# Attention weights of a decoder layer: keys on partitions by a second score product, instead of transposed weights

## What is computed

```python
q = (x @ Wq).reshape(B, T, H, Dh)        # B = 4, T = 512, H = 16, Dh = 32
k = (x @ Wk).reshape(B, T, H, Dh)
v = (x @ Wv).reshape(B, T, H, Dh)
scores = jnp.einsum('bthd,bshd->bhts', q, k)
mask = jnp.tril(jnp.ones((T, T), dtype=scores.dtype))
scores = scores * mask
attn = jax.nn.softmax(scores / T ** 0.5, axis=-1)
out = jnp.einsum('bhts,bshd->bthd', attn, v).reshape(B, T, H * Dh)
return out @ Wo
```

## Time and profile before

| | us |
|---|---|
| median of 3 runs | 1165.44 |
| lowest, highest | 1163.69, 1166.59 |
| profiled execution | 1165.46 |
| its span | 1163.7 |
| TensorE busy | 1053.7 |
| VectorE busy | 777.4 |
| ScalarE busy | 486.3 |
| attention stage, until about | 482 |

### The profile page before, as it was taken

How to read it: one execution, slowest core, us unless ns; L and a number is a source line. 1 busy time by engine, 2 the same in 40 slices (tenths; PEclk the granted TensorE clock), 3 DMA queues, 4 the chain that set the end, 5 groups by cost and what they waited for, 6 DMA issues and landing times.

```text
span 1163.7 us, 18414 instructions
## 1 busy us (share of the span) xinstructions
PE 1053.7 (91%) x6022; PEld 844.8 (73%) x6023; DVE 777.4 (67%) x1920; ACT 486.3 (42%) x934; POOL 251.3 (22%) x431
## 2 busy tenths in 40 slices
PE   2888989898899877499999999999999999999994
PEld 1566767676677665388788888888888888888873
DVE  4678778978987998455664746655465546655666
ACT  4378638854983788122332412221132212221113
POOL 1025324523552353222221001500000000000222
PEclk9989999999999998799999999999999999999997
DMA  5797625752673482222454100510011100100001
GB/s 184 191 303 194 189 90 137 191 145 95 179 192 94 115 234 75 72 64 74 154 171 172 37 1 19 55 37 1 1 37 36 36 0 19 53 1 1 37 37 73
DMA packets 56227, 110.41 MB, mean 95 GB/s; under 512 B 6032, under 2 KB 6032, under 8 KB 56144
## 3 DMA queue, kind: packets, MB, share of 16 engines
q1 hardware_dynamic: 51504, 95.97, 29.4%
q0 software_dynamic: 4640, 13.39, 3.1%
HBM read 72.11 MB, written 35.14 MB: 92 GB/s over the span
## 4 chain that ended last, share of the span: by engine, by line
PE 55%; DVE 2%; issue 0%; ACT 0%; POOLq 0%; POOL 0%; ACTq 0%; DVEq 0%
PE f_bank L42 53%; PE f_bank L1322 1%; PE f_bank L1314 1%; PE f_bank L1364 1%; DVE rows_kept L1661 0%; DVE ln_stats L754 0%; DVE big_hi L1042 0%; DVE hs_lo L1649 0%; DVE ln_mv L756 0%; ACT L767 0%; POOLq L1108 0%; DVE h L1639 0%; ACT hs_hi L1491 0%; POOL out L1276 0%; DVE ln_shift L774 0%
## 5 line engine op out<-in xcount | busy, mean ns | idle before, releaser
L1600 DVE TENSOR_TENSOR h<-f_bank,fsg 128x512 f32<-128x512 f32 x64 | 44.3, 692 | 180.8 <-PE f_bank L42 180.7
L1468 ACT ACTIVATE fsg<-f_bank 128x512 f32<-128x512 f32 x64 | 38.3, 599 | 298.6 <-PE f_bank L42 298.5
L372 PE MATMUL bank<-ident,probs 128*128 128x128 f32 x640 | 124.0, 293 | 42.2 <-ACT probs L489 18.8
L600 DVE CUSTOM_DVE_ANT_0 bank<-bank,mask 128x384 f32<-128x384 f32 (+3 forms) x256 | 126.5, 495 | 32.7 <-PE bank L362 31.0
L489 ACT ACTIVATE probs<-bank,nmax 128x384 f32<-128x384 f32 (+3 forms) x256 | 135.4, 529 | 24.2 <-DVE nmax L610 16.0
L498 ACT ACTIVATE pt_hi<-bank 128x384 f16<-128x384 f32 (+3 forms) x256 | 112.7, 440 | 57.2 <-PE bank L372 51.3
L619 DVE TENSOR_TENSOR pt_lo<-bank,pt_hi 128x384 f16<-128x384 f32 (+3 forms) x256 | 124.8, 488 | 6.0 <-ACT pt_hi L498 5.5
L785 POOL TENSOR_SCALAR ln_var<-ln_mv 128x1 f32<-128x1 f32 x43 | 10.7, 249 | 505.3 <-DVE ln_mv L756 505.3
L42 PE MATMUL bank<-x_hi,w_qk 128*128 128x512 f32 x256 | 97.5, 421 | 23.4 <-DVE x_lo L624 22.3
L372 PEld LDWEIGHTS bank<-ident,probs 128*128 128x128 f32 x640 | 70.9, 144 | 53.8 <-ACT probs L489 33.5
L42 PE MATMUL f_bank<-wd_hi,hs_hi 128*128 128x512 f32 x256 | 100.3, 392 | 3.2 <-DVE rows_kept L1661 3.2
(11 more groups left out here) (220 smaller groups left out, 2449.4 us busy)
## 6 DMA issues: line engine op xcount, KB each, us to landing
big_lo<-q_hi_dram SPq DMA_DIRECT2D x32, 256.0 KB, 4.0
big_lo<-q_lo_dram SPq DMA_DIRECT2D x32, 256.0 KB, 4.8
big_lo<-k_hi_dram SPq DMA_DIRECT2D x32, 256.0 KB, 3.7
big_lo<-k_lo_dram SPq DMA_DIRECT2D x32, 256.0 KB, 5.0
sorted_dram<-z SPq DMA_DIRECT2D x1, 4864.0 KB, 18.1
rows<-sorted_dram SPq DMA_DIRECT2D x19, 256.0 KB, 2.6
x_raw<-x_t SPq DMA_DIRECT2D x4, 1024.0 KB
q_hi_dram<-q_hi SPq DMA_DIRECT2D x16, 256.0 KB, 2.5
```

The costliest lines, as they stand in the source:

```text
L372: ins = pe.transpose(TP[u % TR][:, j * P:(j + 1) * P], probs[u % RP][:, j * P:(j + 1) * P], ident[:, :])
L600: dve.tensor_tensor_reduce(out=S[u % SR][:, 0:cols(r)], in0=S[u % SR][:, 0:cols(r)], in1=mask[:, T - cols(r):T], scale=1.0, scalar=NEG, op ...
L1468: act.activation(fsg[v % 2][:, :], GB[v % 2][:, :], ACT.Silu).then_inc(s_sg, 1)
L1600: dve.tensor_tensor(h[r % 2][:, j, :], UB[v % 2][:, :], fsg[v % 2][:, :], ALU.mult).then_inc(s_h, 1)
```

## The change

The unit becomes the whole head. The scores are computed twice. The first product (`scores`, now in three fills of two PSUM banks) has queries on partitions and serves the row maximum alone: VectorE reduces it by blocks (`maxima`), and once for two heads `row_maxima` finishes the maxima, splits them into two parts and turns them so that they lie along rows. Eight small DMAs on the sync queue (`max_rows`) move them into two more partitions of the stack. The second product (`turned_scores`) has keys on partitions; against the two rows stand rows of -1, so the product itself subtracts the maximum. `exps` then needs no bias, and there are no transposes. `hi` and `lo` work on 1280 columns at once, from SBUF.

Future keys in the diagonal block get -1e30 in both products by a 128-column bfloat16 product of each (`bar_bf` with `ident_bf`), so their weight is zero; in exchange `v_sums` sums v over all later keys, those of the own block too, with 30 products instead of 9 (`later_bf` is a triangle of ones), and `v_above` becomes four copies on ScalarE. The high and low parts use three slots of the stack in place of four, which leaves room for the new rows; the stack is loaded for a pair of heads at a time (`stack_up`, 128 KB a DMA, six for a pair) from DRAM where `put` wrote all heads of a projection.

TensorE is four heads ahead with `scores` and one with `turned_scores`. Six instead of four projections are made before a batch. In the sync queue the fill with zeros now stands after the rows of the first pair (`max_rows(0)`) and before those of the second. The four context loads are issued by ScalarE. `o_tmp` and `v_rest` lie in `z`, with waits for the scatters that read it.

```diff
-    SLOTS = P // HD
+    SLOTS = 3
+    ROWS = SLOTS * HD
     HPT = P // HD
     NM = D // P
-    UPM = HPT * NB
-    UPB = NM * UPM
-    AHEAD_S, AHEAD_MAX, AHEAD_HI, AHEAD_LO, AHEAD_V = 3, 2, -1, -1, -2
-    RP = 4
+    PAIR = 2
+    PPM = HPT // PAIR
+    FILLS = 3
+    AHEAD = 4
+    RING = 4
...
+        v_tail = sb("v_tail", [P, NB, D], F32)
+        KEYS = ((0, 0), (1, T), (3, T + (NB - 1) * P), (2, 2 * T))
+        PW = 2 * T + 2 * P
+        key_at = dict(KEYS)
+        probs = [sb(f"probs{i}", [P, PW], F32) for i in range(2)]
+        pt_hi = [sb(f"pt_hi{i}", [P, PW], F16) for i in range(3)]
+        pt_lo = [sb(f"pt_lo{i}", [P, PW], F16) for i in range(2)]
...
-        S, TP, OB, PJ = bank[0:3], bank[3:5], bank[5:7], bank[7]
-        VB, SF, OT, WB = bank[0:4], (bank[3], bank[5], bank[6]), bank[5:7], (bank[4], bank[7])
-        SR, TR, OR = len(S), len(TP), len(OB)
+        S, ST, OB, PJ = bank[0:2], bank[2:5], bank[5:7], bank[7]
+        VB, OT, WB = bank[0:4], bank[5:7], (bank[7], bank[0])
+        SF = (bank[1], bank[7], bank[6], bank[5])
...
+        starts = {6: 0, 7: 3, 8: 10, 9: 13, 10: 16, 11: 19, 12: 22, 13: 25}
         pieces = {}
-        for g, (first, n) in starts.items():
-            for i in range(0, 3 * KT, n):
-                pieces[first + i // n] = (g, i, i + n)
-        split_at = {first + 3 * KT // n: g for g, (first, n) in starts.items()}
-        x_split_at = {31 + 2 * k: k for k in range(KT)}
-        G_AHEAD = 4
-        between = [("v", 0), ("turn", 0), ("turn", 1), ("v", 2), ("out", 0), ("turn", 2), ("scores", 0), ("out", 1),
+        for g, at in starts.items():
+            pieces[at], pieces[at + 1] = (g, 0, 6), (g, 6, 12)
+        split_at = {at + 2: g for g, at in starts.items()}
+        x_split_at = {6: 0, 7: 1, 8: 2, 9: 3}
...
+            def put(b, m):
+                gm = b * NM + m
+                for side in range(2):
+                    g = gm * 2 + side
+                    for half, done in enumerate((s_pjh, s_pjl)):
+                        sp.wait_ge(done, g + 1)
+                        sp.dma_start(scratch[side][half][m], qk_hl[side][half][:, :].bitcast(F32)).then_inc(s_dw[side], 16)
+            def stack_up(b, i):
+                m, gi = i // PPM, b * NM * PPM + i
+                gm = b * NM + m
+                if i % PPM == 0:
+                    wait_apart(sp, s_passed_sp, [(s_dw[side], (gm + 1) * 32) for side in range(2)])
+                if gi >= RING:
+                    sp.wait_ge(s_ST, FILLS * PAIR * (gi - RING + 1))
+                for side, order in enumerate(((0, 0, 1), (0, 1, 0))):
+                    for slot, half in enumerate(order):
+                        src = scratch[side][half][m].rearrange("(h r) t -> r h t", r=HD)
+                        at = i % PPM * PAIR
+                        sp.dma_start(stack[side][gi % RING][slot * HD:(slot + 1) * HD, :, :].bitcast(F32),
+                                     src[:, at:at + PAIR, :]).then_inc(s_st[gi % RING], 16)
+            def max_rows(gi):
...
+                wait_apart(sp, s_passed_sp, [(s_mt, gi + 1)])
+                for part in range(2):
+                    to = stack[0][gi % RING][ROWS + part:ROWS + part + 1, :, :].rearrange(
+                        "p h (r i n) -> p (h r) i n", r=NB, n=32)
+                    for i in range(P // 32):
+                        at = 32 * i + part * PAIR * NB
+                        sp.dma_start(to[:, :, i, :].bitcast(F32),
+                                     m_rows[gi % 2][at:at + PAIR * NB, :]).then_inc(s_mrow[gi % 2], 16)
...
+                for i in range(PPB):
+                    if i + 4 < PPB:
+                        stack_up(b, i + 4)
+                    elif more:
+                        stack_up(b + 1, i + 4 - PPB)
+                    if i == 1:
+                        put(b, NM - 1)
+                    if i == 3 and more:
+                        sp.wait_ge(s_xl, (b + 2) * KT)
+                        sp.dma_start(x_res, x_rows[b]).then_inc(s_xres, 16)
+                        put(b + 1, 0)
+                    if i in (5, 6) and more:
+                        put(b + 1, i - 4)
+                    if i + 2 < PPB or more:
+                        max_rows(n + i + 2)
...
+            for m in range(2):
+                put(0, m)
+                stack_up(0, 2 * m)
+                stack_up(0, 2 * m + 1)
+            max_rows(0)
             sp.wait_ge(s_const, NCONST)
             tiles = sorted_rows.rearrange("(t p) d -> p t d", p=P)
             zeros = z[0][:, :].unsqueeze(1).broadcast_to([P, sorted_rows.shape[0] // P, D])
             sp.dma_start(tiles, zeros).then_inc(s_zero, 16)
+            max_rows(1)
+            put(0, 2)
...
+            def scores(C, fill):
+                gi, h = C // PAIR, C % PAIR
+                if fill == 0:
+                    pe.wait_ge(s_st[gi % RING], 2 * SLOTS * 16 * (gi // RING + 1))
+                n = FILLS * C + fill
+                if n >= SR:
+                    pe.wait_ge(s_mx, n - SR + 1)
+                to, at = S[n % SR], 0
+                q, k = stack[0][gi % RING], stack[1][gi % RING]
+                for r in ((0, 1), (2,), (3,))[fill]:
+                    w = (r + 1) * P
+                    pe.matmul(to[:, at:at + w], q[0:ROWS, h, r * P:w], k[0:ROWS, h, 0:w], start=True, stop=False)
+                    ins = pe.matmul(to[:, at + r * P:at + w], bar_bf[:, :], ident_bf[:, :], start=False, stop=True)
+                    at += w
+                ins.then_inc(s_S, 1)
+            def turned_scores(C):
+                gi, h = C // PAIR, C % PAIR
+                pe.wait_ge(s_mrow[gi % 2], 8 * 16 * (gi // 2 + 1))
+                q, k = stack[0][gi % RING], stack[1][gi % RING]
+                for fill, keys in enumerate(((0,), (1, 3), (2,))):
+                    if C > 0:
+                        pe.wait_ge(s_e, FILLS * (C - 1) + fill + 1)
+                    for j in keys:
+                        w = T - j * P
+                        at = key_at[j] - fill * T
+                        pe.matmul(ST[fill][:, at:at + w], k[0:ROWS + 2, h, j * P:(j + 1) * P],
+                                  q[0:ROWS + 2, h, j * P:T], start=True, stop=False)
+                        ins = pe.matmul(ST[fill][:, at:at + P], ident_bf[:, :], bar_bf[:, :], start=False, stop=True)
+                    ins.then_inc(s_ST, 1)
+            def values(C):
...
+                for r in reversed(range(NB)):
+                    chain = [(j, part) for j in range(r, NB) for part in (V0, V1, V2)]
+                    for n, (j, part) in enumerate(chain):
+                        ins = pe.matmul(SF[r][:, :], (later_bf if j == r else ones_bf)[:, :],
+                                        v3[:, j, :, part:part + HD], start=(n == 0), stop=(n == len(chain) - 1))
                     ins.then_inc(s_sf, 1)
...
+                for c in range(HEADS):
+                    C = b * HEADS + c
+                    ahead = more or c + AHEAD < HEADS
+                    if c < HEADS - 1:
+                        turned_scores(C + 1)
+                    if c == 0:
+                        pe.wait_ge(s_sfe, (b + 1) * NB)
                         pe.wait_ge(s_z, PRIMED + b * NB)
-                    if u < UPB:
-                        transposes(b, u)
-                    if u + AHEAD_S < UPB:
-                        scores(b, u + AHEAD_S)
-                    if u in pieces and (more or pieces[u][0] < 2 * NM):
-                        project(b, *pieces[u])
-                    if u + AHEAD_V >= 0:
-                        values(b, u + AHEAD_V)
+                    if ahead:
+                        scores(C + AHEAD, 0)
+                        scores(C + AHEAD, 1)
+                    if runs(more, 2 * c):
+                        project(b, *pieces[2 * c])
+                    if ahead:
+                        scores(C + AHEAD, 2)
+                    if runs(more, 2 * c + 1):
+                        project(b, *pieces[2 * c + 1])
+                    values(C)
...
+            pe.wait_ge(s_sfe, NB)
+            for C in range(AHEAD):
+                for fill in range(FILLS):
+                    scores(C, fill)
+                if C % 2 == 1:
+                    project(0, 4 + C // 2, 0, 3 * KT)
+            turned_scores(0)
...
+            def exps(C):
+                if C >= 2:
+                    act.wait_ge(s_lo, C - 1)
+                for fill in range(FILLS):
+                    w = min(T, PW - fill * T)
+                    act.wait_ge(s_ST, FILLS * C + fill + 1)
+                    act.activation(probs[C % 2][:, fill * T:fill * T + w], ST[fill][:, 0:w], ACT.Exp).then_inc(s_e, 1)
+            def hi(C):
+                act.wait_ge(s_e, FILLS * (C + 1))
+                if C >= 3:
+                    act.wait_ge(s_pv, C - 2)
+                act.activation(pt_hi[C % 3][:, :], probs[C % 2][:, :], ACT.Copy).then_inc(s_hi, 1)
...
+            def maxima(C):
```

(38 more changed lines are left out.)

347 lines of the change are left out of this document (147 added, 200 removed).

## The result

The changed kernel takes 1314.7 us (median of four runs, 1312.1 to 1319.0) against 1164.6: ratio 1.129 [1.1255, 1.1324]. The forecast was 1213.5 with a range of 1170 to 1255. The sign was right, the size was not.

The account below looks back on a forecast made before the run. TensorE paced loops with projections and VectorE those without; the change adds a wait for row maxima moved by small DMAs. First batch 26.8, later batches 4.7, 5.1 and 10.8, between loops 0.6: 48.0 on 1165.44 gives 1213.5 us, range 1170 to 1255.

Parts of the forecast that it names:

- step 5: Row cycle, sync queue: eight small DMA issues 0.43 us apart (bounds 0.2 and 0.47), the last starting 3.1 us later.
- Head on TensorE: TensorE's work per head: two score products, bars at 0.06 us each and value products, 3.12 us, 0.4 more than before.
- VectorE, 3.7 a head: VectorE's maxima, row maxima and subtraction: 3.7 us per head against 3.9 before, no gain that counts.
- dip of 1.6: Low-clock allowance of 1.6 us added to each two-head cycle without projections, making 9.8 us 11.4.
- Step 6: Row cycle: landing of the last small DMA, taken as 1.8 us, bounds 1.4 and 3.
- Steps 1 to 4: Row cycle from TensorE's release through scores, maxima and small VectorE instructions: done at 4.85 us, 5.8 with half a projection.
- First batch: Zero fill delays the second pair's rows, TensorE standing until 87.0; loop ends at 165.4 instead of 138.6, +26.8 us.
- Between loops: Longer tail sums less a stall and dip that go: net +0.2 us, three times 0.6 in all.
- A: Rival: row DMAs are cheap, issues at 0.25 us and no clock dips; 1168 to 1198, middle 1190; chance 0.20.
- B: Rival: path from row maxima to stack is covered, rows landing within 3.2 us; 1160 us; chance 0.13.
- C: Rival: clock falls in every one of some 24 cycles; 1235 to 1275, middle 1255; chance 0.17.
- D: Rival: removed transposes' 1.0 us a head frees no TensorE time, 1.4 us of products replacing it; in all cases, no chance given.

Follow-up runs that it names:

- x12: x7 plus five unread 512-column products into the free projection bank ahead of the third score fill, in steps without projections; 1211.6 us.
- x15: x12 without the bar products in both score products, so future keys count as well; 1189.2 us.
- x6: Changed kernel with the split of a finished projection moved ahead of ScalarE's exponentials and VectorE's maxima; 1289.2 us.
- x16: Changed kernel with x6's moved split, x12's added products and x5's early zero fill; four heads ahead, eight small DMAs a pair; 1288.7 us.
- x14: x16 with four small DMAs a pair instead of eight, only the high part of the row maxima moved; 1231.2 us.
- x13: x11 with the tail sums over one of the three parts of v, 10 products instead of 30; 1202.9 us.
- x11: x8 plus unread products in steps without projections, four small DMAs a pair (high part only) and the early zero fill; 1221.2 us.
- x7: x6's moved split on the changed kernel with row maxima not moved into the stack, a constant subtracted instead; 1219.8 us.
- x5: Changed kernel with the zero fill issued ahead of the constants and the first rows; 1306.5 us.
- x8: Changed kernel with x6's moved split and scores six heads ahead instead of four; 1249.5 us.
- x3: Changed kernel plus 8 unread 512-column products (14 in the last batch) on TensorE before each row wait; 1336.2 us.

## Why the prediction was wrong, point by point

Two things failed: the issue of a small DMA was taken too short (step 5), and the wait for the projection bank behind VectorE's new order was in no term. Where the clock is high and no context load is in flight, the other steps of the cycle are near the forecast. The steps down, each line's kernel against the one above it (x12 and x15 do not compute the reference):

| Kernel | us | from the line above |
|---|---|---|
| changed | 1314.7 | |
| no bank stall (x6) | 1289.2 | -25.5 |
| TensorE kept busy, fill early (x16) | 1288.7 | -0.5, two effects cancel |
| four DMAs a pair (x14) | 1231.2 | -57.5 |
| no rows moved, fill in its place (x12) | 1211.6 | -19.6 |
| no bars (x15) | 1189.2 | -22.4 |
| before | 1164 | -25 |

Of the last 25 us the tail sums are 18.3 by x13, measured on x11. The last 7 were not taken apart.

- **Head on TensorE, 3.12 us**: right within 0.2, though a bar costs 0.09 to 0.1 and not 0.06. A step with half a projection (1.4 us) takes 4.35 in x7, which leaves 2.95; one with a whole (2.8) takes 5.83, which leaves 3.03. So with the stalls gone about half of the steps with projections are TensorE bound, as the sum had it; those in which the projection begins behind the third fill take 4.98, with a wait for a score bank in them.
- **VectorE, 3.7 a head**: right. The steps that stay at 4.1 without bars too (step 3) are its own, and in the others it keeps up with 3.5.
- **Step 5, issues at 0.43**: the step that failed. They stand 0.68 us apart, with a few gaps up to 1.0, so 5.4 to 5.7 us for eight and not 3.5, outside my bounds of 0.2 to 0.47. I took the value from loads of many rows, and reasoned that fewer rows could only be cheaper. Over seven spacings that is 7 x (0.68 - 0.43) = 1.75 us a cycle. It can be read straight off x16's second loop: the five cycles from 222.73 to 285.64 take 62.9 us where the forecast had 54.2 (9.8 + 11.4 + 10.7 + 12.5 + 9.8), 1.7 more each on average (the second of them holds 1.1 us of added products, where the forecast had a dip of 1.6). By the forecast's 24 cycles an estimate of 42 us. That their number is the price is shown by x14: half of them, 57.5 us less.
- **Step 6, landing 1.8 from the start of the last issue**: right in the loops with projections: 1.7 in five of the changed kernel's seven waits there, 2.4 and 2.6 in the first batch. In the last loop it was 3.3 to 4.4 in the four cycles with a context load in flight: an estimate of 8 us in all. The forecast had priced these loads as time on ScalarE's queue (0.4 us each by the trace) and not as company for the small DMAs.
- **Steps 1 to 4, turning at 4.85 (5.8 with half a projection)**: 5.1 to 6.0 in x16's second loop, apart from the cycle that holds the added products (6.8), so right within 0.5 at the high clock. In the changed kernel's last loop it is 6.1, of which the dip of 1.6 was in the sum; 7.7 and 8.3 come where the low clock and other stalls meet it, and the low clock of the loops with projections (0.85) was in no term.
- **VectorE's new order, in no term**: the prediction says what is queued behind the row wait, but not what stands behind the row maxima on VectorE. I counted the row maxima as time on VectorE (1.1 us, no gain that counts) and not as 1.1 us, with the maxima of a whole head, in front of the split that frees the projection bank. That is the term that is missing altogether: 25 us in the changed kernel, 53 without rows (x6 and x7, which move the split on ScalarE too). With the 42 and 8 us above and the 10 between the loops it makes some 86 of the 101 us between forecast and result; the rest was not taken apart, and as the waits hide each other the terms need not add up.
- **First batch**: the fill does delay the second pair, but it was worth 8 us (x5), not 15. The stall ended at 85.56, forecast 87.0.
- **Between loops, +0.2**: measured +3.7. The terms named there make +0.6, not +0.2. The tail sums' 4.6 us came as forecast; the stall that goes (2.4) is all that came off, the 0.66 and the dip of 1.5 lay in the loop, and the clock is 0.96 there, an estimate of 32.75 x 0.04 = 1.3 us.
- **Rivals**: A is excluded, its issues at 0.25 us are nowhere met. B's condition, small DMAs that land in 3.2 us, is not met either, but two more heads cover the path whole (x8, no row wait) and B's time of 1160 does not come: 1249.5, and 1211.6 in x12, without rows. B had loops with projections at 75.3 us, in x12 they take 84, and the last 69.5 for 65. C had a mechanism that I gave too small a chance: the clock falls in loops with projections too (0.85, and 0.63 in the last). Alone it is not shown to be the excess: x12 gains 8 us by it without rows, and x3 had a higher clock and a longer time. D, that the exchange frees no TensorE time, holds: bars and tail sums are 41 us of work (x15 and x13).

The forecast's signs of being right nearly all came (the row wait in the last loop, the stall behind the fill, the clock below 0.95), but the second and third loops take 104 us and not 80 to 85, and the small DMAs stand 0.68 us apart and not 0.4. The named mechanism was there; it was priced too low, and a second one stood beside it.

What stays open: how much of the excess is the low clock's doing, since the row wait could not be had without its stall; whether the context loads hold up the small DMAs of the last loop, which a run that issues them elsewhere would tell; and why a small DMA's issue takes half as long again as a large one's.

## What to carry to other kernels

Two stalls that stand in one in-order queue hide each other: taking one away shows only the difference, so remove the second as well before you price the first (the rows were worth 42 us with the bank stall in place, 69 without it). An edit made to cure one kernel can hurt the next: the products that won 8 us without rows lost as much in the last loop with them. When a change makes the unit of work coarser, list for every engine what now stands in front of each instruction that frees a buffer. Before you move a value through many tiny DMAs, count their issues in a row on the path, and take the time of one from a DMA of that size. Here a second queue shortened that path and cost the engine that issued on it.

## What the runs showed of the hardware

- A DMA of 1 KB (eight rows of 128 bytes) from SBUF to SBUF held the sync queue and ScalarE's 0.68 us from one issue to the next, with a few gaps of 0.8 to 1.0 us, while a 128 KB load took mostly 0.43 to 0.47.
- TensorE was released by the last of eight such DMAs 1.05 to 1.09 us after the end of its issue in 16 of x16's 23 waits. With a 1 MB load issued from ScalarE's queue among them it was 2.5 to 3.3 us (x16), 2.7 to 3.8 (changed kernel) and, with four small DMAs, 4.0 to 5.1 (x14).
- TensorE at the low clock can stay there while busy: 14.8 of 15 us busy at 0.50 in x7, with small products and their weight loads. Before it fell it had stood 1.33 us. In x12, with wide products in the same gaps, it stayed at 1.00 at 13.4 to 14.0 of 15 us busy.
- A bfloat16 product of 128 columns between wider ones cost 0.09 us (x12 to x15), where the start of the row behind it comes after 0.04.
